# Longer strings of identity transposes ahead of three stages of a macaron block, and short ones behind their first transposes

## What is computed

```
x = L0_attn_x
x = x + 0.5 * ffn(layernorm(x))        # 2 choices of 8 experts
x = x + attn(layernorm(x))             # 16 heads, xPos rotation, decay mask
x = x + 0.5 * ffn(layernorm(x))        # the same weights
```

```
scores = softmax(xf @ router_w); weights, experts = top_k(scores, 2)
for k in range(2):                     # capacity = tokens / 8 per expert
    h = gelu(xe @ w1[e]); y = h @ w2[e]
    out += scatter_back(y) * weights[:, k]
```

## Time and profile before

| | us |
|---|---|
| median of 3 runs | 2301.62 |
| lowest, highest | 2299.54, 2303.91 |
| the profiled execution | 2323.99 |
| its span, first to last instruction | 2322.2 |
| its mean granted TensorE clock | 0.974 |

### The profile page before, as it was taken

How to read it: one execution, slowest core, us unless ns; L and a number is a source line. 1 busy time by engine, 2 the same in 40 slices (tenths; PEclk the granted TensorE clock), 3 DMA queues, 4 the chain that set the end, 5 groups by cost and what they waited for, 6 DMA issues and landing times.

```text
span 2322.2 us, 57931 instructions
## 1 busy us (share of the span) xinstructions
PE 2182.2 (94%) x22549; PEld 1919.0 (83%) x22549; DVE 1358.6 (59%) x3312; ACT 1003.4 (43%) x2149; POOL 1179.5 (51%) x911
## 2 busy tenths in 40 slices
PE   7869999999999997999999999849999999999998
PEld 6759999999999986777777777639999999999997
DVE  7755555555555552568878877545555555555553
ACT  4434434343434442445555555434343443444442
POOL 5765777735454533223344453354777754444443
PEclk9999999999999998999999999769999999999999
DMA  9523444434343424002211121123444443434432
GB/s 365 207 80 67 98 93 90 107 82 103 80 104 82 102 57 118 28 33 75 74 43 59 58 76 75 59 77 97 102 89 102 89 101 86 100 87 98 88 80 32
DMA packets 138440, 211.52 MB, mean 91 GB/s; under 512 B 34092, under 2 KB 114544, under 8 KB 132080
## 3 DMA queue, kind: packets, MB, share of 16 engines
q0 software_dynamic: 57344, 69.21, 18.2%
q1 hardware_dynamic: 80912, 139.72, 17.7%
HBM read 138.13 MB, written 72.88 MB: 91 GB/s over the span
## 4 chain that ended last, share of the span: by engine, by line
PE 52%; DVE 5%; issue 3%; ACT 1%; another core or an unknown queue 0%; POOL 0%; POOLq 0%; DMA 0%; DVEq 0%; ACTq 0%
PE bank L674 16%; PE bank L663 15%; PE bank L756 10%; PE bank L844 3%; PE bank L877 2%; PE bank L812 1%; PE bank L644 1%; PE bank L827 1%; PE bank L862 1%; PE bank L916 1%; PE bank L774 1%; DVE aw L1817 0%; DVE rt L1805 0%; DVE xnl L1791 0%; DVE lnr_mv L1458 0%
## 5 line engine op out<-in xcount | busy, mean ns | idle before, releaser
L1155 ACT ACTIVATE h<-bank 128x512 f32<-128x512 f32 x512 | 306.7, 599 | 858.1 <-PE bank L663 687.5
L1726 DVE CAST hh<-h 128x512 fp32r<-128x512 f32 x512 | 240.5, 470 | 700.0 <-ACT h L1155 621.2
L674 PE MATMUL bank<-w2h,hh 128*128 128x256 f32 x2048 | 582.3, 284 | 3.1 <-ACT yb L1173 3.1
L674 PE MATMUL bank<-w2h,hl 128*128 128x256 f32 x2048 | 579.5, 283 | 0.0
L674 PE MATMUL bank<-w2l,hh 128*128 128x256 f32 x2048 | 579.3, 283 | 0.0
L674 PEld LDWEIGHTS bank<-w2h,hh 128*128 128x128 f32 x2048 | 391.0, 191 | 22.3 <-ACT yb L1173 3.9
L663 PE MATMUL bank<-xh,w1h 128*128 128x512 f32 x1024 | 407.0, 397 | 1.7 <-DVE xl L1713 1.7
L663 PE MATMUL bank<-xl,w1h 128*128 128x512 f32 x1024 | 406.1, 397 | 0.0
L674 PEld LDWEIGHTS bank<-w2l,hh 128*128 128x128 f32 x2048 | 391.4, 191 | 16.4
L663 PE MATMUL bank<-xh,w1l 128*128 128x512 f32 x1024 | 400.2, 391 | 0.0
L674 PEld LDWEIGHTS bank<-w2h,hl 128*128 128x128 f32 x2048 | 391.2, 191 | 0.0
(11 more groups left out here) (215 smaller groups left out, 3315.0 us busy)
## 6 DMA issues: line engine op xcount, KB each, us to landing
stg<-in_L_ffn_w SPq DMA_DIRECT2D x64, 1024.0 KB
xb<-acc SPq DMA_DIRECT2D x9, 1024.0 KB, 7.8
xa<-in_L_attn_x SPq DMA_DIRECT2D x8, 1024.0 KB, 13.9
xn_rows<-xa SPq DMA_DIRECT2D x8, 1024.0 KB
xn_rows<-xn_r SPq DMA_DIRECT2D x8, 1024.0 KB
xr<-acc SPq DMA_DIRECT2D x7, 1024.0 KB
out_rows<-xr SPq DMA_DIRECT2D x7, 1024.0 KB
slot_table<-pay,idx POOLq DMA_INDIRECT x256
```

The lines of the kernel that those rows point to most:

```text
L674: last = pe.matmul(o, a[:, fj, s], c[:, fj, :], start=(fj == 0 and n == 0 and (end or t % 2 == 0)), stop=(fj == FJ - 1 and n == 2), skip_g ...
L1155: act.activation(h32[fj % 2][:], bank[fj % 2][:], ACT.Gelu_apprx_tanh).then_inc(f.gelu, 1)
L1726: dve.tensor_copy(hh[:, fj, :], h32[fj % 2][:]).then_inc(f.hh, 1)
```

## The change

The two uses of 27 identity transposes become 51 in the first feed-forward and 39 in the second (`TURNS`), and 35 ahead of attention. Six more are put behind the first group's 8 transposes in each feed-forward, and eight more behind `front_pair(0, 0)` in attention. Nothing else moves, and no wait is added or taken away: 64 transposes more in all (24 + 12 + 8 in the strings that were there, 6 + 6 + 8 in new places). They write banks 0 and 7, which hold nothing at those points, and count no semaphore.

```
+            def turn_over(o, count):
+                for n in range(count):
+                    pe.transpose(o[:, 0:P], ident, ident)
...
-                warm_up()
+                pe.wait_ge(f.rows0, 16)
+                turn_over(bank[0], TURNS[r])
                 transposes(0, GT * 16, None)
+                turn_over(bank[0], 6)
                 pe.wait_ge(f.w1l, FJ)
...
                 last.then_inc(full, 1)
+                if b == 0 and j == 0:
+                    turn_over(bank[7], 8)
...
             pe.wait_ge(A.x, 16)
-            for n in range(WARM):
-                pe.transpose(bank[7][:, 0:P], ident, ident)
+            turn_over(bank[7], 35)
...
-WARM = 27
+TURNS = (51, 39)
```

More of the change, by code:

```diff
@@ L645, in transposes @@
                         last.then_inc(f.xT, 1)
-                def warm_up():
-                    pe.wait_ge(f.rows0, 16)
-                    for n in range(WARM):
-                        pe.transpose(bank[0][:, 0:P], ident, ident)
                 def up(j, fj, up_free, by_half=False):
```

## The result

| | kernel before | changed kernel |
|---|---|---|
| median of 18 runs, us | 2301.68 | 2304.74 |
| lowest, highest | 2296.35, 2305.47 | 2301.64, 2310.35 |
| ratio, 95% interval | 1 | 1.0017 [1.0010, 1.0023] |

The forecast was 2296.1 with a range up to 2302.0. The time lies outside it, on the other side of the kernel before. The loss is small, 0.17%, but the interval excludes no change, and also the gain.

What follows compares the result with a forecast made beforehand. The prediction took TensorE's work at full clock, plus what the joints between stages cost, as the bound. Savings of 2.8 + 1.3 + 1.4 = 5.5 us off 2301.62 gave 2296.1, range 2291.5 to 2302.0.

Steps and rivals of the forecast that it cites:

- First feed-forward, -1.3 us: First feed-forward's start: saves 2.2 us if the clock stays up, 0.3 if not; the middle, 1.3, was taken.
- a sign of being wrong: Behind a string: the group's transposes start without a wait, so the string outlasted its pause; no size given.
- the lower end of my term: First feed-forward: if the clock falls in the pause ahead of the rows, only 0.3 us is saved, an estimate.
- Attention's start, -1.4 us: From the second front pair through `project(0)`: full clock there saves 1.4 us on the way to `turn(0)`.
- Second feed-forward, -2.8 us: Second feed-forward's first up-projections: at full clock, the sixteenth matmul starts 3.5 us after the first, not 6.29; saves 2.8 us.
- The added transposes while they lie in a pause: nothing: All three joints: the longer strings and short strings fit into TensorE's waits and cost 0 us.
- Rival (4): TensorE's "issue" waits: 128 more instructions to fetch, one more wait with its clock fall costs 6.4 us, 2302.5; chance 0.07.
- A rule against the change: All strings: the Trainium skill says transposes aren't granted full clock, which would make the sum a loss; a small chance kept.
- Rival (1): All three joints: strings don't raise the clock and outlast their pauses, 4.0 us lost, 2305.6; chance 0.05.
- (2): Clock doesn't hold over first feed-forward's pause nor the wait ahead of `turn(0)`: 3.1 us gained, 2298.5; chance 0.16.
- (5): All joints: runs without a profile lack the stretches at 1.2 GHz, so nothing changes, 2301.6; chance 0.02.
- (3): Attention's later clock falls: one more (2299.5) or one fewer (2292.7), up to 3.4 us each; chance 0.20, half each way.

Runs made afterwards that it cites:

- e8: The kernel before, unchanged, run again for a trace on a chip of the 2301 us kind: 2301.81 us, ratio 1.0000.
- e4: The changed kernel, unaltered, run again beside the kernel before on one chip of the 2301 us kind: 2303.76 us, ratio 1.0018 to the kernel before.
- e10: The changed kernel plus 41 small matmuls (82 entries) ahead of attention's string, a shift of 128 in all: 2300.52 us, ratio 0.9989 to the kernel before.
- e5: The changed kernel with the last batch's four bias additions moved from GpSimd to VectorE: 2300.90 us, ratio 0.9999 to the kernel before.
- e11: The changed kernel with both the bias additions on VectorE and 82 entries ahead of attention's string: 2296.26 us, ratio 0.9981 to the kernel before.
- e15: The changed kernel without its second feed-forward part, plus 82 entries ahead of attention's string, on a 2320 us chip: 2317.49 us, ratio 0.9991 to the kernel before.
- e12: The kernel before plus 128 entries of small matmuls ahead of attention's string, on a 2320 us chip: 2319.00 us, ratio 1.0001.
- e1: The kernel before with only the change's first feed-forward part, on a 2320 us chip: 2317.74 us, ratio 0.9984.
- e0: The kernel before, unchanged, run again for a second trace on a 2320 us chip: 2321.06 us, ratio 1.0003.
- e9: The kernel before plus 23 float32 matmuls (46 entries) in TensorE's pause ahead of attention, on a 2301 us chip: 2304.55 us, ratio 1.0014.
- e6: The kernel before with only the last batch's four bias additions moved from GpSimd to VectorE: 2304.26 us, ratio 1.0009.

## Why the prediction was wrong, point by point

**First feed-forward, -1.3 us: right in size and mechanism.** Against e8 the stage was 1.6 us shorter in the result's trace, 1.0 in e4 and 1.9 in e10, and the clock was 1.00 from 139.03 us on. Two details differed. The rows came 7.6 us after the string's start where the trace I read had 9.8, so in e4, e5, e10 and e11 the string of 51 outlasted the pause, in e4 by some 0.6 us: the group's transposes started without a wait, which I had named as a sign of being wrong, and the stage still gained. And where they came late, in e15, the clock fell, as the lower end of my term has it; the 0.3 us that I gave that end had no row behind it, and e15's stage, 778.0 us, is 1.3 us longer than e12's, not shorter. Nor is the kind of chip all of it: in e1 the rows were there 7.7 us after the string's start. I had read the lengths of pauses from one execution on the slower kind of chip and carried them over; the cover of 1.1 us that I counted was not there.

**Attention's start, -1.4 us: right, where the joint is cold.** 8.80 - 7.17 = 1.6 us. `turn(0)` came 7.17 us after the front pair, predicted 7.4; the wait ahead of it grew to 1.41 us, predicted 1.7, and the clock survived it. In e0 the kernel before had its 7.17 us without the change, so the gain isn't there in every execution.

**Second feed-forward, -2.8 us: the first step that failed.** Measured +0.1 to +1.8 us. The joint did its part: after a first step of 0.31 us the up-projection matmuls came every 0.23 us, at a clock of 1.00 from 1531.67, and the sixteenth started 3.49 us after the first, predicted 3.5. What failed is a sentence in the first part, that the loads and conversions inside a feed-forward "are released by TensorE's own progress, so they move along". POOL's additions start when its eight gathers are issued, 11.1 us after the string's start with and without the change, whatever TensorE does, and they hold DVE. I counted sixteen matmuls and stopped there, at the end of the cold stretch, without asking what the later ones need: the twenty-fifth, first of the fifth up-projection, needs a bank that ACT frees, which waits for `hl`, which waits for the cast. The sign was in the trace of before:

```profile
1562.03 5.00 POOL L406 TENSOR_TENSOR xb<-xb,hbias 128x512 f32<-128x512 f32 x4
...
1564.28 3.03 DVE L1726 CAST hh<-h 128x512 fp32r<-128x512 f32 x1 [3.11 <-ACT h L1155]
```

A cast of 3.03 us beside additions of 5.00 us, where e5's takes 0.52, ended in time there only because TensorE was slow. With e5's edit the term is -2.5 us, close to the 2.8.

**"The added transposes while they lie in a pause: nothing": the second step that failed.** They cost nothing where they stand, but they move the code behind them by 46 entries, and the sum has no term for that. As a rival the waits for instructions were named, priced, and given too little. Rival (4) had late instructions as its mechanism and 2302.5 as its time, with a chance of 0.07. The mechanism was theirs, but not as I had it: not 128 more instructions to fetch, since 82 more entries made e10 faster, but other instructions at the fixed places. Its size is +2.7 us by e9, by the sums of waits +2.8 us, and 0.0029 and 0.0018 of the time by e10 against e4 and e11 against e5, 6.7 and 4.1 us. It was not a question of chance either: four waits at those places in every trace with a shift of 46. Had I taken the distances between the "issue" waits in the trace of before, I could have laid them over the new order of TensorE's instructions. That shows which instructions are hit, though not, without a run, what each costs.

**A rule against the change: refuted here.** The Trainium skill's "TensorE: Matmul & The Clock Gate", Part 4, has no full clock for transposes. In the changed kernel the clock is 1.00 from 913.86, 5.8 us into a string of nothing but transposes, and no joint was lost to it. Rival (1) is out. So is (2) on the 2301 us chips, since the clock held over both pauses it named, and (5), since the time changed. (3), a changed number of falls within attention, is not what lengthened it: between 940 and 1460 us the result's trace has 6.8 us at a clock of 0.50, e9's 6.8 and e8's 10.2.

**Readings of mine that were off.** Two falls of the clock lie inside a wait and not behind it: at 925.01, 0.96 us before the wait of 1.63 us ends, and at 989.86, 0.82 us before the one of 3.01 us ends. And the low end of the range by my own terms is 2292.7 - 0.9 = 2291.8, not 2291.5. Neither touches the argument.

**The sum.** By trace and run, on a chip of the result's kind: -1.6 (first feed-forward) - 1.6 (attention's start) + 1.2 (second, mean of +1.7, +0.1 and +1.8) + 2.7 to 6.7 (places) = +0.7 to +4.7 us. Measured: +3.1. The terms come from single traces and from medians with intervals of about 2 us each way, so they agree no better than that. e11 turns two of the terms around, and its -5.6 us is what the three joints were forecast to give, 5.5. That it fits so closely is partly luck: in the traces of e8 and e11 the stages differ by 1.4, 0.2 and 2.5 us, 4.1 in all.

**Left open.** Why chips differ, and whether a shift of 46 costs anything on the 2320 us kind, where it wasn't run; the shifts of 16 and 30 did no harm there. Why some instructions cost more than others at a fixed place. Why e6's median was higher, and what e1 gained by.

## What to carry to other kernels

When a stretch gets faster, follow the chain on to the first instruction that depends on another engine, and look for long entries there that were covered by the slowness: an elementwise instruction that takes several times its usual duration beside a GpSimd instruction is one. For differences of a few tenths of a per cent, give each edit a twin that shifts TensorE's later code by as much and does nothing else, and one that shifts it back; without e9 and e10 I would have blamed the joints, which worked. And read the pause that a filler is to fill on more than one chip, since it was 7.6 us here and 9.8 there. A wait marked "issue" can be held against the packets of the instruction queue before it is called unexplained.

## What was not expected of the hardware

- In attention, TensorE's waits marked "issue" of over 0.5 us end 1.2 to 1.6 us after a 16 KB packet of the instruction queue landed, 97 of 97 in 18 traces. They stand whole multiples of about 124.6 of PE's entries apart, last up to 4.2 us, and at the same instruction are of different length in each execution.
- A DVE cast from SBUF to SBUF of 0.52 us took 2.5 to 4.4 us beside GpSimd's additions, and ended 0.3 us after them.
- A float32 matmul of 128x8 was recorded as two entries of 0.215 us each (19.77 us for 92).
